# One fused AdaLN + state-space + FFN kernel: the low part of the dt series moves ahead of the variance, and the last stage and the FFN softmax are reordered

## What is computed

```python
x = x + attn(cond(x, cond_128, ...), in_proj_w, conv_weight, ...)      # a Mamba-2 like layer
x = x + ffn(cond2(x, cond_128, ...), weight, bias, centroids, assignments)
# attn: proj = h @ in_proj_w.T -> gate, x|B|C (causal conv of 4 taps, silu), dt
#   dt_p = softplus(dt + dt_bias);  state = state*exp(dt_p*A) + dt_p*x (outer) B;  y = state . C + x*D
#   yn = y * rsqrt(mean(y*y over a group of 512) + eps) * norm_weight * silu(gate);  out = yn @ out_proj_w.T
# ffn:  dots = softmax(x @ centroids.T / 0.1);  hits = dots > 0.01
#   out = where(any(hits, 1)[:, None] & any(hits, 0)[assignments][None, :], x @ weight.T + bias, 0)
```

## Time and profile before

| | before |
|---|---|
| median of 3 runs | 1619.86 us (1619.21 to 1621.07) |
| the profiled execution | 1624.18 us, span 1622.4 us |
| PE busy | 1594.5 us (98%), 13001 matmuls |
| DVE / ACT / POOL busy | 1055.4 / 846.1 / 774.1 us (65 / 52 / 48%) |
| granted clock of the PE, mean | 0.998 |
| DMA read / written | 82.64 / 8.45 MB |

### The profile page before, as it was taken

The page is one execution under the profiler, slowest core; times in us unless marked ns, Lnnn a source line. Parts: engine busy times, 40 slices in busy tenths (PEclk is TensorE's granted clock), DMA queues, the critical chain, the costliest instruction groups (busy, mean ns, idle before and its releaser), DMA issues. The chain is left out here.

```text
span 1622.4 us, 32566 instructions
## 1 busy us (share of the span) xinstructions
PE 1594.5 (98%) x13001; PEld 1279.6 (79%) x13001; DVE 1055.4 (65%) x1741; ACT 846.1 (52%) x1372; POOL 774.1 (48%) x731
## 2 busy tenths in 40 slices
PE   9999999999999999999999999999999999999997
PEld 6778888888888888877787888888888888887665
DVE  4877666665656666676786656565666666565456
ACT  3654556555555555555455655555454655554321
POOL 3564545546363644544345554636464554543203
PEclk9999999999999999999999999999999999999999
DMA  5110201111111102011012111111010201115782
GB/s 184 59 53 21 59 21 58 35 53 40 40 53 34 49 15 63 27 53 40 30 43 73 53 40 46 47 34 60 33 40 21 65 27 53 41 36 116 190 187 105
DMA packets 50294, 93.19 MB, mean 57 GB/s; under 512 B 5664, under 2 KB 6304, under 8 KB 50144
## 3 DMA queue, kind: packets, MB, share of 16 engines
q1 hardware_dynamic: 50144, 91.11, 19.5%
HBM read 82.64 MB, written 8.45 MB: 56 GB/s over the span
## 5 line engine op out<-in xcount | busy, mean ns | idle before, releaser
L487 PE MATMUL PS<-xh,wh 128*128 128x512 f32 x1280 | 519.6, 406 | 0.0
L487 PE MATMUL PS<-xh,wl 128*128 128x512 f32 x1280 | 499.8, 390 | 0.0
L487 PE MATMUL PS<-xl,wh 128*128 128x512 f32 x1280 | 499.8, 390 | 0.0
L522 DVE SCALAR_TENSOR_TENSOR cb<-PS,P,cb 128x496 f32<-128x496 f32 (+2 forms) x576 | 412.5, 716 | 132.4 <-ACT cb L508 118.8
L184 POOL TENSOR_TENSOR wl<-rw,wh 128x512 fp32r<-128x512 f32 x160 | 212.2, 1331 | 191.6 <-ACT wh L179 191.6
L726 POOL TENSOR_TENSOR ysum<-yq 128x256 f32<-128x256 f32 x128 | 109.5, 856 | 362.3 <-ACT yq L711 362.2
L487 PEld LDWEIGHTS PS<-xh,wl 128*128 128x128 f32 x1280 | 240.3, 188 | 52.9
L487 PEld LDWEIGHTS PS<-xh,wh 128*128 128x128 f32 x1280 | 240.6, 188 | 50.7 <-ACT wh L179 0.5
L487 PEld LDWEIGHTS PS<-xl,wh 128*128 128x128 f32 x1280 | 241.1, 188 | 44.4
L508 ACT ACTIVATE cb<-PS,P 128x512 f32<-128x512 f32 x192 | 148.4, 773 | 204.9 <-PE PS L487 204.9
L775 PE MATMUL PS<-oh,yh 128*128 128x512 f32 x512 | 200.1, 391 | 3.2 <-POOL yl L735 3.2
(11 more groups left out here) (201 smaller groups left out, 2184.1 us busy)
## 6 DMA issues: line engine op xcount, KB each, us to landing
rw<-in_w_in SPq DMA_DIRECT2D x160, 256.0 KB, 2.7
ro<-in_w_out SPq DMA_DIRECT2D x64, 256.0 KB, 2.8
x2s<-acc SPq DMA_DIRECT2D x16, 260.0 KB, 5.3
out_x<-acc SPq DMA_DIRECT2D x16, 256.0 KB, 2.4
acc<-in_x SPq DMA_DIRECT2D x3, 1024.0 KB, 9.9
wh<-x2s SPq DMA_DIRECT2D x8, 260.0 KB, 3.4
wl<-x2s SPq DMA_DIRECT2D x8, 260.0 KB, 6.4
wh<-x2s SPq DMA_DIRECT2D x8, 259.5 KB, 4.2
```

The lines of the kernel that those rows point to most:

```text
L487: fn = lambda e, k=k, w=w, v=v, i=i: e.matmul(PS[:, bank, :], w[:, m, 128 * k:128 * k + 128], v[:, k, a:a + 512], start=(i == 0), stop=(i ...
L522: dve.op(lambda e, d=d, w=w: e.scalar_tensor_tensor(out=cv[:, :, d:32], in0=pv[:, :, 0:32 - d], scalar=w, in1=cv[:, :, d:32], op0=ALU.mult ...
```

## The change

Four parts. (1) In the passes that turn the dt series, the low part `al` becomes a function of its own, `DT_low`, and stands on DVE ahead of `rstd` and `add_out` of the last tile; on POOL `avh` (which needs only `ah`) stands ahead of the power of `rstd`, and `avl` behind it. (2) `turn` writes its tile to two PSUM banks in turn and waits for the low part of tile T-2, not T-1. (3) In the softmax the division of the 64 values, the maximum with `pmx` and the maximum of a row become one operation: `pmx = max(ex * rc, pmx)`, and the row's test is made on `rc` itself, since the largest `ex` of a row is 1; the dense half stands ahead of the wait for the exponential. (4) `last_products` has another order: both convolutions first, y of tiles 0 and 1 together ahead of `A_dve` and `M_dve`, y of tiles 2 and 3 behind `Y`, and the FFN weights' split behind the first `add_out` pair.

```diff
@@ -451,6 +451,11 @@
             act.wait("DT", b)
             act.op(lambda e: e.copy(turned(dtt), dt), "dtt", b)
             act.op(lambda e: e.copy(turned(ah), av_), "ah", b)
+
+        def DT_low(b):
+            a = 4 * (b % 2)
+            turned = lambda t: t[:, a:a + 4, :].rearrange("p (r i) c -> p i r c", r=2)
+            av_ = PS[:, SEG[0], 256:512].rearrange("p (i r c) -> p i r c", i=2, r=2)
             dve.wait("ah", b)
             dve.op(lambda e: e.tensor_tensor(turned(al), av_, f(turned(ah)), ALU.subtract), "alo", b)
 
@@ -548,15 +553,16 @@
             c = P_D + 4 * g + j
             act.op(lambda e: e.mul(xsd[:, j, :], xs[:, j, :], P[:, c:c + 1]), "xsd", (n, j))
 
-        def av(n):
+        def av(n, parts=(0, 1)):
             half, g, tb = who(n)
             b = 2 * half + tb
             pool.wait("dtt", b)
             pool.wait("ah", b)
-            pool.wait("alo", b)
             if n >= 1:
                 pool.wait("O", (n - 1, 3))
-            for src, dst, kind in ((ah, avh, "avh"), (al, avl, "avl")):
+            for src, dst, kind in [((ah, avh, "avh"), (al, avl, "avl"))[k] for k in parts]:
+                if kind == "avl":
+                    pool.wait("alo", b)
                 pool.op(lambda e, src=src, dst=dst: e.tensor_tensor(
                     dst.rearrange("p (i h t) -> p i h t", i=4, h=8),
                     bc(f(src[:, 4 * tb:4 * tb + 4, 8 * g:8 * g + 8]).rearrange("p i (h o) -> p i h o", o=1), 128, 4, 8, 32),
@@ -842,6 +848,11 @@
                     X_dve(4 * block_at[n + 1] + m - 6)
                 if b is not None and m in (2, 4):
                     X_dve(4 * b + 1 + m // 2)
+                turned_now = n == 0 or n - 1 in block_at
+                if m == 6 and turned_now:
+                    assert not chain
+                    DT_low(block_at[n - 1] if n else 0)
+                    av(n, (0,))
                 if prev:
                     when = dict(O=(1, 3, 4, 5), acc=(2, 5, 5, 6))
                     at = lambda kind: [i for i in range(4) if when[kind][i] == m]
@@ -867,7 +878,6 @@
                         add_out(n - 1, i)
                 if m == 3 and not prev:
                     G_mask(n)
-                turned_now = n == 0 or n - 1 in block_at
                 if m == 6 and not turned_now:
                     av(n)
                 if n == 0 and m == 6:
@@ -890,10 +900,9 @@
                 evac(n, m)
                 if m == 6 and turned_now:
                     t = block_at[n - 1] if n else 0
-                    assert not chain
                     DT_pe(t, [("acc", (n - 1, 1)) if n else ("xl", 5)])
                     DT_split(t)
-                    av(n)
+                    av(n, (1,))
                 if n == 0 and m < 6:
                     split_w_hi(0, m + 4)
                     split_w_lo(0, m + 4)
@@ -1077,12 +1086,12 @@
 
         def turn(T):
             pe.wait("x3", T)
-            if T >= 1:
-                pe.wait("x3l", T - 1)
+            if T >= 2:
+                pe.wait("x3l", T - 2)
             else:
-                pe.wait("dtx", (end_n, 3))
+                pe.wait(*(("dtx", (end_n, 3)), ("var", (end_n, 3)))[T])
             for k in range(4):
-                fn = lambda e, k=k: e.transpose(PS[:, PT, 128 * k:128 * k + 128], xs[:, T % 2, 128 * k:128 * k + 128], ident)
+                fn = lambda e, k=k: e.transpose(PS[:, (PT, PG)[T % 2], 128 * k:128 * k + 128], xs[:, T % 2, 128 * k:128 * k + 128], ident)
                 pe.op(fn, "xt", T) if k == 3 else pe.op(fn)
 
         def x3_split(T):
@@ -1091,9 +1100,9 @@
                 act.wait("O", (end_n, 3))
             elif T >= 3:
                 act.wait("ff", (T - 3, 0))
-            act.op(lambda e: e.copy(x3_slot(True, T), PS[:, PT, :]), "x3h", T)
+            act.op(lambda e: e.copy(x3_slot(True, T), PS[:, (PT, PG)[T % 2], :]), "x3h", T)
             dve.wait("x3h", T)
-            dve.op(lambda e: e.tensor_tensor(x3_slot(False, T), PS[:, PT, :], f(x3_slot(True, T)), ALU.subtract), "x3l", T)
+            dve.op(lambda e: e.tensor_tensor(x3_slot(False, T), PS[:, (PT, PG)[T % 2], :], f(x3_slot(True, T)), ALU.subtract), "x3l", T)
 
         FB = ((SEG[0], PP[2]), PY)
 
@@ -1143,28 +1152,26 @@
             dve.wait("ff", (T, 1))
             if T >= 1:
                 dve.wait("fn", T - 1)
-                dve.wait("q", T - 1)
             dve.op(lambda e: e.tensor_reduce(s4[:, 0:1], lgt, AX.X, ALU.max), "fm", T)
             dve.wait("fm", T)
             dve.op(lambda e: e.tensor_scalar(nm, s4[:, 0:1], -10.0, None, ALU.mult), "fn", T)
             act.wait("fn", T)
             if T >= 2:
                 act.wait("pm", T - 2)
-                act.wait("qm", T - 2)
             act.op(lambda e: e.activation(ex[:, r, :], lgt, ACT.Exp, bias=nm, scale=10.0, accum_out=sx), "se", T)
             dve.wait("ld_bf", 0)
             if T < LATE:
                 dense(T, 0)
-            dense(T, 1)
+            if T < NT - 1:
+                dense(T, 1)
+            dve.wait("se", T)
             dve.op(lambda e: e.reciprocal(rc, sx), "frc", T)
             dve.wait("frc", T)
-            dve.op(lambda e: e.tensor_scalar(ex[:, r, :], ex[:, r, :], rc, None, ALU.mult), "pp", T)
-            dve.wait("pp", T)
             dve.wait("pm", T - 1)
-            dve.op(lambda e: e.tensor_tensor(pmx, pmx, ex[:, r, :], ALU.max), "pm", T)
-            dve.op(lambda e: e.tensor_reduce(s4[:, 1:2], ex[:, r, :], AX.X, ALU.max), "qm", T)
-            dve.wait("qm", T)
-            dve.op(lambda e: e.tensor_scalar(qs[:, T:T + 1], s4[:, 1:2], 0.01, None, ALU.is_gt), "q", T)
+            dve.op(lambda e: e.scalar_tensor_tensor(out=pmx, in0=ex[:, r, :], scalar=rc, in1=pmx, op0=ALU.mult, op1=ALU.max), "pm", T)
+            dve.op(lambda e: e.tensor_scalar(qs[:, T:T + 1], rc, 0.01, None, ALU.is_gt), "q", T)
+            if T == NT - 1:
+                dense(T, 1)
             dve.wait("q", T)
             if T >= LATE:
                 return
@@ -1199,45 +1206,48 @@
         def last_products():
             n = end_n
             conv2(0)
-            y_dve(n, 0)
-            y_high(n, 0)
-            y_low(n, 0)
-            y_square(n, 0)
+            conv2(1)
+            conv2_last_tap(0)
+            for i in (0, 1):
+                y_dve(n, i)
+                y_high(n, i)
+                y_low(n, i)
+                y_square(n, i)
             y_sum(n, 0)
+            y_sum(n, 1)
             A_dve(n, 2)
             A_dve(n, 3)
             M_dve(n, 2)
             M_dve(n, 3)
-            for i in (1, 2, 3):
-                y_dve(n, i)
-                y_square(n, i)
-                y_sum(n, i)
-                y_high(n, i)
-                y_low(n, i)
-            weights2(0)
-            weights2(1)
+            x3_act(0)
+            x3_act(1)
+            load_G(4)
+            load_G(5)
             O(n, 0)
             Y(n, 2)
             Y(n, 3)
             O(n, 1)
             S(n, (0, 1))
-            conv2(1)
-            conv2_last_tap(0)
-            x3_act(0)
-            load_G(4)
-            load_G(5)
+            turn(0)
             O(n, 2)
-            turn(0)
             O(n, 3)
             S(n, (2, 3))
+            for i in (2, 3):
+                y_dve(n, i)
+                y_high(n, i)
+                y_low(n, i)
+                y_square(n, i)
+            y_sum(n, 2)
+            y_sum(n, 3)
             x3_split(0)
-            weights2(2)
-            weights2(3)
-            x3_act(1)
-            for tiles in sums(n):
-                rstd(n, tiles)
-                for i in tiles:
-                    add_out(n, i)
+            rstd(n, (0, 1))
+            add_out(n, 0)
+            add_out(n, 1)
+            for k in range(4):
+                weights2(k)
+            rstd(n, (2, 3))
+            add_out(n, 2)
+            add_out(n, 3)
 
         for n in range(NS):
             stage(n)
@@ -1257,7 +1267,6 @@
         dve.op(lambda e: e.tensor_scalar(csel, bc(sm[:, 40:41], 64, 128), 0.01, None, ALU.is_gt), "cs", 1)
         pe.wait("cs", 1)
         pe.wait("oh1", 0)
-        pe.wait("var", (end_n, 3))
         pe.op(lambda e: e.matmul(PS[:, PG, :], csel, ohf, start=True, stop=True), "rsel", 0)
         pe.op(lambda e: e.matmul(PS[:, PT, :], csel, ohf, start=True, stop=True), "rsel2", 0)
         for T in range(LATE + 1, NT):
```

## The result

| | before, beside it | changed |
|---|---|---|
| median | 1619.13 us (1618.71 to 1621.07, 6 runs) | 1614.39 us (1613.01 to 1618.86, 6 runs) |
| ratio, 95% interval | | 0.9972 (0.9961 to 0.9983) |
| the profiled execution, span | 1624.18, 1622.4 us | 1618.86, 1617.1 us |
| mean granted clock in it | 0.998 | 0.995 |

The change makes the kernel 4.7 us faster, where 5.5 was forecast. Run again beside a `before` of 1621.2, the same kernel gave 1616.74 (0.9976, 0.9966 to 0.9985), 4.5 us faster.

A forecast was written before the change was run, and what follows sets the result against it. PE, busy in 98% of the span, was taken to bound the kernel. Turning passes -0.7, last stage +3.4 and FFN +2.8 summed to 5.5 us, so 1619.9 became 1614.4, with an 8 in 10 range of 1611.0 to 1617.4.

The forecast's parts named there:

- passes 1, 16 and 17: Turning passes: `seg` waits go in 1 and 17, +1.0 and +1.3; pass 16 loses 2.5 through a late load.
- The row of 2.19: Profile row of pass 0: an `ol` begun while POOL spreads takes 2.19 instead of 0.74; used to forecast pass 16.
- pass 0: First turning pass: `seg` wait goes, but `ol` is blocked and `A(0, 1)` starts later: -0.5, bounds -1.5 and +0.5.
- ACT comes 1.0 later: Pass 0: blocked `ol` of row 0 frees its load 1.5 later, ACT comes 1.0 later, `A(0, 1)` starts at 75.2.
- the last stage: Part 4: waits ahead of output products 0 and 1 go, product 2 waits 0 to 0.7: +3.4, bounds +1.5 and +3.8.
- the FFN: Parts 2 and 3, behind tile 10: shorter DVE circle and second bank give +2.8, bounds +1.4 and +3.7.
- the change takes the dense half (0.31) off this circle: FFN, DVE's work per tile: without dense half, multiplication and row maximum with its gap, 2.84 becomes about 2.05.
- the tail: From the selection on, POOL works without a pause and its list is unchanged, so this stretch only moves: 0.
- rival (d): Clock falls to half rate behind new PE pauses, 1.5 each, 1 to 3 times: 1617.5, no change; chance 0.12.
- (a): Turning passes: loads of pass 16 have slack or `ol` precedes `avl`; part 1 gives +1.5 to +2.8: 1611.4; chance 0.17.
- (b): Last stage refilled by 2 us waits, ACT sets the DVE circle; parts 2 to 4 give 3.7: 1616.9; chance 0.18.
- (c): Slower: variance behind the spread costs each of four turning passes 2.5, 10 in all: 1623.7; chance 0.03.

The follow-up runs named there:

- e9b: Changed kernel with part 1 in passes 1 and 17 only, and POOL waiting for `al` ahead of `avh` in passes 0 and 16: 1613.04 us, 0.9946.
- e1: Changed kernel with part 1 in passes 1 and 17 only, but `avh` still not waiting for `al`: 1614.39 us, 0.9957.
- e3: Changed kernel with `oh` of rows 2 and 3 behind the exponentials on ACT in passes 0 and 16: 1611.61 us, 0.9944.
- e5: Changed kernel, passes 0 and 16: `ol` of row 0 ahead of DVE's low part, `oh` of rows 2 and 3 behind ACT's exponentials: 1612.26 us, 0.9944.
- e11b: The kernel of e5 run once more, beside the changed kernel on one chip: 1610.55 us, 0.9941.
- e6: Changed kernel with part 4 undone (the old `last_products`): 1620.14 us, 0.9996.
- e7: Changed kernel with part 3 undone (the old softmax, `ffn_ops`), two PSUM banks kept: 1618.70 us, 0.9988.
- e2: Kernel before with part 1 alone (the `DT_low` and `av` hunks), in all four turning passes: 1621.81 us, 1.0019.
- e10b: The changed kernel run again, unedited, beside a `before` of 1621.2: 1616.74 us, 0.9976.
- e4: Changed kernel with `ol` of row 0 ahead of the dt series' low part on DVE in passes 0 and 16: 1610.84 us, 0.9943.
- e8: Changed kernel with part 2 undone (old `turn` and `x3_split`, one PSUM bank), new softmax kept: 1617.57 us, 0.9978.

## Why the prediction was right, and where it was not

**Right, with its size: passes 1, 16 and 17.** Forecast +1.0, -2.5, +1.3, measured +1.07, -2.54, +1.33 where the clock stayed. Pass 16 went by the forecast's own steps: DVE behind the power, `ol` held by `avl`, `oh` waiting 4.15 for its load (forecast 3.5, and a start at 811.3 on before's scale; it was 809.56 in an execution that stood 1.63 ahead there, so 811.2), `A(16, 1)` released by L411. The row of 2.19, from another pass, carried it. e9b and e1 show what the contention alone is worth, at the same order of operations: 109.27 without it, 110.31 with it. By the Trainium skill, page "GPSIMD Engine Reference", section "Key points", VectorE operations with two SBUF inputs contend with GpSimd's; e9b and e1 agree for `ol`. The section gives no size, which here is from 0.3 (1.05 instead of 0.74) to the whole of POOL's operation.

**Right in sign, its size open: pass 0.** Forecast -0.5, measured -0.11 against the profiled execution of `before` and -0.66 against e9b, which has the same order there. `avl` held the small chain operation ahead of `ol` (1.38 instead of 0.23), and `ol` of row 0 began 1.55 later behind `A(0, 0)` than in `before`, as forecast. `oh` of row 2 came 1.37 later. But the next `oh`, which before waited 0.36 for its own load, waited no more, and L411 started only 0.66 later (10.96 behind `A(0, 0)` where it was 10.30; in e9b it is 9.77). The step that this puts in doubt is "ACT comes 1.0 later": it is 0.7 against the one and 1.2 against the other, and the forecast lies between. My statement that `A(0, 1)` could gain 0.5 at most took L411 as given; with ACT's order changed (e3, e5, e11b) the stretch is 10.3 to 10.6 instead of 12.

**Right: the last stage.** +3.4 forecast, 3.52 and 3.16 measured, 3.5 in e6. Output product 0 would start at 1498.8, product 1 at 1502.8 and product 2 at 1506.5 on before's scale; `A(30, 1)` stands 1.05 later in the changed execution, and 1499.59, 1503.62 and 1507.73 less 1.05 are 1498.54, 1502.57 and 1506.68. The new wait is 0.27, within the 0 to 0.7.

**Mis-sized: the FFN, 2.8 forecast, 2.11 measured.** The step that failed is "the change takes the dense half (0.31) off this circle". It doesn't. `dense` itself waits for the exponential where c is 1 (`dve.wait("se", T)` in its body, which the diff doesn't touch); the moved call changed nothing, which the row at 1593.20 and its old twin show: 0.47 of idle time in front of each. 2.05 + 0.31 = 2.36, and 2.37 was measured. Two or three such circles make 0.6 to 0.9 of missing gain. Only tile 15, whose dense half was put behind the maximum, is rid of it.

**Not foreseen: the tail, +0.7.** I said that it only moves. From POOL's last addition to the end of the span it was 3.25 before and 2.53 after; e7 and e2, both with the old softmax, have 3.25 and 3.15 as well, and the other profiled executions, all with the new one, 2.46 to 2.54. So the difference goes with the softmax, but by which way it reaches the last store is open.

**Half right: the clock.** As rival (d) I gave 0.12 to the case that the clock falls behind the new wait, at 1.5 each. The price was exact (47.4 against 45.9), the pause shorter than forecast (1.78 and 1.92, not 2.5). That it is a matter of the single execution I did not think of: at least 22 of 56 have it. The gain is 5.4 in an execution without a fall and 4.5 and 4.7 in the medians; that the fall makes this difference is my reading, since the start moves them as well. The Trainium skill, page "TensorE: Matmul & The Clock Gate", section "Why this matters for your kernels", says that an idle gap that is long enough brings half rate; the traces agree that a gap does it, and show that this one sometimes does and sometimes doesn't.

**Luck in the last digit.** 1614.4 was forecast and 1614.39 measured, but from a median of `before` that is 0.7 above that of the six runs beside the result, and with errors that cancel: in e10b's column 0.65 too much for the FFN, 0.24 for the last stage, and 0.41 that the ordinary passes cost without a reason that I know, against 0.74 at the tail and 0.4 in pass 0 (by the one execution of `before`) that I had not counted on; and about 1 for the clock.

Of the rivals, (a) was refuted in pass 16 by the wait of 1.78, but its gain can be had by other orders: with `ol` of row 0 in front and ACT's `oh` behind the exponentials (e11b) the kernel takes 1610.55 us, 0.9941 of the time before, and e3 and e9b are level with it in the stretches. (b) and (c) are refuted by the last stage and by passes 1 and 17.

## What to carry to other kernels

Before an operation is moved, list what the engine does next for somebody else: here the wait that went from pass 0 was 1.7 us at `seg` and worth nothing, and the ones that came stood behind a load that a delayed VectorE operation released. Of a call that moves, read the body, for a wait inside it moves with it. And an engine that works in order should not stand at a load ahead of work that PE is due to wait for: put what waits for the transfer behind it, even if the load is there most of the time.

## What the runs showed of the hardware

- A VectorE operation with two SBUF inputs that started while GpSimd worked on SBUF ended behind GpSimd's (1.67 and 2.19 where it takes 0.74 alone, and 4.55 for two that met two): `ol` of e4 ends at 801.79 and `avl` at 801.25, the second `ol` of e1 at 805.52 and `avl` at 804.97, so some 0.5 of it was still to be done. Where it started first by 0.3 us, it took 0.74 and GpSimd's took 2.20 instead of 1.92. VectorE's `dtx` and `al`, which read one input from PSUM, kept their 0.6 to 0.7 and 0.42 beside it.
- A pause of PE of 1.7 to 2.0 us at `A(0, 1)` and `A(16, 1)` was followed by about 3 us at half clock in some executions and by none in others, of one and the same kernel.
- The start differs from one execution to the next. PE's timelines, of the kernel before, of the changed one (two rows) and of e4:

```profile
23.29 0.79 PE L355 MATMUL PS<-ab,xb 64*128 64x512 f32 x1
...
6.05 1.66 PE L208 MATMUL PS<-yh 128*128 128x512 f32 x6
...
37.84 0.65 PE L630 MATMUL PS<-big 128*32 128x32 f32 x32 [3.36 <-ACT big L547]
...
36.22 0.46 PE L630 MATMUL PS<-big 128*32 128x32 f32 x32 [0.46 <-ACT big L547]
```

  Until 23.3 a product of 512 columns took 0.79 in the one, and products started 0.23 apart only from 28.9 on; in the changed one it was so from 6 (six products in 1.66, where e4 and e11b, which came to it near 14, have 2.93). The granted clock reads 1.00 in all these windows of `before`, so only the rows show the half rate. The start up to `A(0, 0)` was longest where full rate came last, 62.7 us. But earliest was not best: in the seven executions that had it by 11 and then waited 3.3 to 3.4 at L630 (the changed one, e1, e3, e5, e6, e8, e9b), the granted clock fell to 0.50 from about 36 to 43, and `A(0, 0)` came at 60.4 to 60.9. The four that had it near 14 (e2, e4, e7, e11b) waited 0.5 to 1.7 there without a fall, and it came at 57.5 to 58.3. e10b, with full rate by 9.4 and a wait of 1.68, had a short fall and 57.6. So the changed kernel alone differs by 2.8 us in its start, and all kernels by up to 5.
